# Two groups of eight heads instead of four groups of four for the products with values, and one copy for each

## The reference

```python
def _L0_xattn_ref(query, key, value, wq, wk, wv, wo):      # 16 heads of width 16
    q = (query @ wq.T).reshape(B, S, H, dk_h).transpose(0, 2, 1, 3)
    k = (key @ wk.T).reshape(B, S, H, dk_h).transpose(0, 2, 1, 3)
    v = (value @ wv.T).reshape(B, S, H, dv_h).transpose(0, 2, 1, 3)
    scores = jnp.einsum('bhqd,bhkd->bhqk', q, k) / scale
    attn = jax.nn.softmax(scores, axis=-1)
    out = jnp.einsum('bhqk,bhkd->bhqd', attn, v)
    out = out.transpose(0, 2, 1, 3).reshape(B, S, d_value)
    return out @ wo.T

x = x + jnp.tanh(g_xattn[0]) * _L0_xattn_ref(_layernorm(x), ctx_1024, ctx_1024, ...)
x = x + jnp.tanh(g_ffn[0]) * _L0_ffn_ref(_layernorm(x), ...)
x = x + jnp.tanh(g_xattn[1]) * _L1_xattn_ref(ctx_1024, _layernorm(x))    # an alignment by dynamic programming
x = x + jnp.tanh(g_ffn[1]) * _L1_ffn_ref(_layernorm(x), ...)
```

## Time and profile before

| | |
|---|---|
| median of 3 runs | 1828.75 us (1828.48 to 1829.92) |
| the profiled execution's own time | 1828.01 us |
| its span, first to last instruction | 1826.2 us |
| mean granted clock of TensorE over the span | 0.874 |
| busy in the span | PE 77%, DVE 78%, ACT 61%, POOL 30% |

### The profile page before, as it was taken

One profiled execution on the slowest core, in us unless ns is written; L12 is line 12 of the kernel. 1 busy time (PEld: TensorE's weight loads), 2 busy tenths in 40 slices (PEclk: granted clock), 3 DMA queues, 4 the chain that ended last, 5 costly groups with the idle time before them and its releaser, 6 DMA issues. The chain is left out here.

```text
span 1826.2 us, 35776 instructions
## 1 busy us (share of the span) xinstructions
PE 1414.0 (77%) x10821; PEld 1072.6 (59%) x10821; DVE 1420.9 (78%) x4062; ACT 1107.6 (61%) x2395; POOL 551.6 (30%) x998
## 2 busy tenths in 40 slices
PE   5899999999999999999999986133332004899896
PEld 4578788888887888878888765000001002566664
DVE  6677777777777777777777642899998998999996
ACT  3476676676766767667677662243335002999997
POOL 3122222322222223222233221200000002778785
PEclk8899999999999999999999997555555555999999
DMA  5444445444444444444543310322220002222321
GB/s 175 139 129 116 138 125 146 121 116 140 124 135 124 117 142 130 118 129 123 147 123 107 111 42 18 99 59 61 60 45 11 0 0 81 76 87 92 100 76 47
DMA packets 322936, 179.49 MB, mean 98 GB/s; under 512 B 93793, under 2 KB 318193, under 8 KB 322802
## 3 DMA queue, kind: packets, MB, share of 16 engines
q1 hardware_dynamic: 322802, 178.07, 35.0%
HBM read 122.91 MB, written 50.33 MB: 95 GB/s over the span
## 5 line engine op out<-in xcount | busy, mean ns | idle before, releaser
L982 DVE TENSOR_REDUCE nmax<-s 128x2 f32<-128x512 f32 x512 | 327.0, 681 | 7.9 <-PE s L454 6.9
L709 ACT ACTIVATE pt<-s 128x512 f32<-128x512 f32 x512 | 281.0, 611 | 70.0 <-PE s L471 69.9
L1074 POOL TENSOR_TENSOR r<-rl 128x512 f32<-128x512 f32 x128 | 133.1, 1040 | 328.4 <-ACT rl L739 285.6
L454 PE MATMUL s<-kst,qst 96*128 96x256 bf16 x1024 | 158.2, 275 | 11.6 <-DVE nmax L982 8.0
L471 PE MATMUL s<-qst,kst 128*128 128x256 bf16 x1024 | 156.9, 275 | 1.1 <-ACT pt L709 0.8
L1341 PE MATMUL gate<-diag,one 128*128 128x512 f16 x35 | 21.3, 608 | 171.7 <-DVE left L1432 171.7
L739 ACT ACTIVATE rl<-wb,fscl 128x256 f32<-128x256 f32 x256 | 107.8, 476 | 64.7 <-PE wb L555 64.7
L551 PE MATMUL wb<-x2l,wfcT 128*128 128x256 f32 x512 | 143.3, 302 | 0.7 <-ACT dd L761 0.7
L485 PE MATMUL oacc<-pt,vw 128*32 128x256 f32 x2048 | 137.0, 385 | 6.4 <-ACT pt L709 6.0
L951 DVE TENSOR_TENSOR r2l<-r,r2h 128x512 fp32r<-128x512 f32 x128 | 88.6, 692 | 65.2 <-POOL r L1074 40.3
L418 PE MATMUL wb<-wprT,r2l 128*128 128x256 f32 x512 | 131.8, 296 | 6.9 <-DVE r2l L951 6.9
(11 more groups left out here) (270 smaller groups left out, 3951.9 us busy)
## 6 DMA issues: line engine op xcount, KB each, us to landing
kst<-k_parts_dram SPq DMA_DIRECT2D x384, 64.0 KB, 2.5
qst<-q_parts_dram SPq DMA_DIRECT2D x384, 64.0 KB, 2.4
k_parts_dram<-kp SPq DMA_DIRECT2D x32, 384.0 KB, 5.2
q_parts_dram<-qp SPq DMA_DIRECT2D x32, 384.0 KB, 3.1
xin<-in_x_dram SPq DMA_DIRECT2D x32, 256.0 KB, 2.8
cT<-in_ctx_T_dram SPq DMA_DIRECT2D x32, 256.0 KB, 2.7
xres<-in_x_dram SPq DMA_DIRECT2D x32, 256.0 KB, 3.1
cin<-in_ctx_dram SPq DMA_DIRECT2D x32, 256.0 KB, 4.6
```

The costliest lines, as they stand in the source:

```text
L454: last = pe.matmul(s1[h % 2][:, t, :], qst[b.p][0:MAXROW, h, t * P:t * P + P], kst[b.p][0:MAXROW, h, :], start=True, stop=True)
L709: act.activation(pt[h % (2 * HPG)][:], s2[h % 2][:], ACT.Exp).then_inc(e["expd"], 1)
L982: v.tensor_reduce(nmax[:, T * h:T * h + T], s1[h % 2][:], AX.X, ALU.max, negate=True)\
L1074: pool.tensor_tensor(r2[:], rl[:, k % 2], rl[:, k % 2], ALU.mult)\
```

## The change

`values` takes eight heads at once: two groups of four, 16 matmuls (32 records) one after the other, into both halves of `oacc`. It is called twice in an iteration, where groups 1 and 3 stood; the calls for groups 0 and 2 are gone from their places. `copy_half` empties both halves of `oacc` with one instruction of 512 columns, where `copy_group(i, 1)` and `copy_group(i, 3)` stood. The semaphores' counts follow: the exponentials of a half of the heads wait for the products of the half that last used the `pt` tiles.

```diff
-            def values(b, g):
-
-                w("expd", NH * b.n + HPG * (g + 1), NH * NB)
-                if g == 0:
+            def values(b, half):
+                w("expd", NH * b.n + NH // 2 * (half + 1), NH * NB)
+                if half == 0:
                     if at(b, 0):
                         pe.wait_ge(e["w_made"], GPR_MADE)
                     w("vw_cp", b.n + 1)
-                w("o_cp", NG * b.n + g, NG * NB)
-                for t in range(T):
-                    for j in range(HPG):
-                        last = pe.matmul(oacc[HW * j:HW * j + HW, g % 2, :], vw[b.p][:, t, HPG * g + j, :],
-                                         pt[(HPG * g + j) % (2 * HPG)][:, t, :],
-                                         start=(t == 0), stop=(t == T - 1))
+                w("o_cp", 2 * b.n + half, 2 * NB)
+                for g in range(2):
+                    for t in range(T):
+                        for j in range(HPG):
+                            last = pe.matmul(oacc[HW * j:HW * j + HW, g, :], vw[b.p][:, t, NH // 2 * half + HPG * g + j, :],
+                                             pt[HPG * g + j][:, t, :], start=(t == 0), stop=(t == T - 1))
                 last.then_inc(e["av_mm"], 1)
...
                 if there(i):
-                    values(i, 0)
                     scores2(i, 4, 6)
...
                 if there(i):
-                    values(i, 1)
+                    values(i, 0)
...
                 if there(i):
-                    values(i, 2)
                     scores2(i, 14, 16)
...
                 if there(i):
-                    values(i, 3)
+                    values(i, 1)
...
             def exps(b, lo, hi):
                 for h in range(lo, hi):
                     w("s2_mm", NH * b.n + h + 1, NH * NB)
-                    w("av_mm", NG * b.n + h // HPG - 1, NG * NB)
+                    w("av_mm", 2 * b.n + h // (NH // 2), 2 * NB)
...
-            def copy_group(b, g):
-                w("av_mm", NG * b.n + g + 1, NG * NB)
-                w("o_t", 2 * (b.n - 1) + g // 2 + 1, 2 * NB)
-                act.activation(osb[:, g, :], oacc[:, g % 2, :], ACT.Copy).then_inc(e["o_cp"], 1)
+            def copy_half(b, half):
+                w("av_mm", 2 * b.n + half + 1, 2 * NB)
+                w("o_t", 2 * (b.n - 1) + half + 1, 2 * NB)
+                act.activation(osb[:, 2 * half:2 * half + 2, :], oacc[:], ACT.Copy).then_inc(e["o_cp"], 1)
```

More of the change, by code:

```diff
@@ L481, in values @@
                     w("vw_cp", b.n + 1)
-                w("o_cp", NG * b.n + g, NG * NB)
-                for t in range(T):
-                    for j in range(HPG):
-                        last = pe.matmul(oacc[HW * j:HW * j + HW, g % 2, :], vw[b.p][:, t, HPG * g + j, :],
-                                         pt[(HPG * g + j) % (2 * HPG)][:, t, :],
-                                         start=(t == 0), stop=(t == T - 1))
+                w("o_cp", 2 * b.n + half, 2 * NB)
[4 more added lines that the diff above has]
+                                             pt[HPG * g + j][:, t, :], start=(t == 0), stop=(t == T - 1))
                 last.then_inc(e["av_mm"], 1)
             def turn_o(b, half):
-                w("o_cp", NG * b.n + 2 * half + 2, NG * NB)
+                w("o_cp", 2 * b.n + half + 1, 2 * NB)
                 if half == 0:
@@ L698, in values_copy @@
                     act.wait_ge(e["pool_set"], VALUES_SET)
-                w("v_mm", b.n + 1), w("av_mm", NG * (b.n - 1), NG * NB)
+                w("v_mm", b.n + 1), w("av_mm", 2 * (b.n - 1), 2 * NB)
                 for t in range(T):
@@ L782, in iteration @@
                 if there(i):
-                    copy_group(i, 0)
                     exps(i, 4, 6)
@@ L797, in iteration @@
                 if there(i):
-                    copy_group(i, 1)
+                    copy_half(i, 0)
                 if there(y):
@@ L816, in iteration @@
                 if there(i):
-                    copy_group(i, 2)
                     exps(i, 14, 16)
@@ L822, in iteration @@
                 if there(i):
-                    copy_group(i, 3)
+                    copy_half(i, 1)
                 if there(z):
```

## The result

The changed kernel takes 1869.96 us (median of 4 runs, 1869.31 to 1874.01) against 1828.62 us before (4 runs, 1827.05 to 1829.92). The ratio is 1.0231, with a 95% interval of 1.0213 to 1.0249: slower, by 41 us. The prediction was 1871 us.

The account below looks back on a forecast made before the run. PE looked like the bound, but the moved groups were taken to fill its waits for DVE and ACT. +1.38 us a batch, 42.4 in all, on 1828.0 gave 1870.4; the median stands 0.7 higher, so 1871 us, range 1857 to 1878.

Parts of the forecast that it names:

- Price of a group and of a block: On PE: a group costs 1.11 us, 0.25 of it entering and leaving the narrow form; a 32-record block costs 1.93.
- First place: Group 0's old place, between queries and `scores2` of heads 4 and 5: PE waits for `yn` and `xh`, +0.52 us a batch.
- Second place: Group 2's old place, between heads 13 and 14: PE waits for ACT's exponentials, so removal gains 0.00 us a batch.
- The block at the end: Groups 2 and 3 joined where group 3 stood: same start, 0.86 us longer, later PE work shifts by +0.86 a batch.
- The sum: +1.38 us a batch, 38.6 over batches 2 to 29, 3.2 for 30 and 31, about +0.6 for 0 and 1: 42.4.
- Busy time: Sign: PE's busy time from 600 to 800 us falls to 94 or 96%, at a clock still 1.00.
- The first rival: Both places have slack and PE keeps what it is spared: 0.50 us less a batch, 1813 us; 5 in 100.
- The third rival: `copy_half` becomes exposed, `turn_o` or `distance` waits: up to 0.59 us a batch more, 1890 us; 4 in 100.

Follow-up runs that it names:

- The second merge alone: Kernel before, with only groups 2 and 3 joined in one block with one copy, groups 0 and 1 unchanged: 1855.12 us, ratio 1.0139.
- the copies alone: Kernel before, all four groups left in place, each two emptied by one 512-column copy behind the second: 1829.46 us, ratio 0.9997.
- the work done twice: Changed kernel, with heads 0 to 3 and 8 to 11 also multiplied at the places groups 0 and 2 left: 1881.53 us, ratio 1.0279.
- the block cut in two: Changed kernel, with heads 8 to 11 moved from the second block to ahead of `fc(z, 2)`, one copy kept: 1879.53 us, ratio 1.0295.
- the new order with one merge and with both: Groups 2 and 3 joined, or changed kernel with DVE's `yn` earlier; `fc(z, 2)` before scores of heads 14 and 15, other orders moved: 1827.46 and 1825.64 us.
- the earlier turn in each of these: Both reordered kernels, one merge and both, with `turn_x(a)` put ahead of `turn_o(z, 1)`: 1828.26 us with one, 1828.29 us with both.
- the four groups in the new order: Orders of the 1828.29 us kernel, with four groups and four copies, group 2 ahead of `fc(z, 2)`: 1842.77 us, ratio 1.0073.
- the kernel that met both: The 1828.29 us kernel (both merges, reordered, `turn_x` earlier), with DVE's `split_max(s)` moved behind `low_squares(z, 2)`: 1812.17 us, ratio 0.9910.
- two long blocks in the same new order: Changed kernel with DVE's `yn` and `xh` earlier, `fc(z, 2)` and other orders moved, and `turn_x` ahead of `turn_o`: 1828.29 us, ratio 0.9993.

## Why the prediction was right

It said 1871 us with a range of 1857 to 1878; measured were 1870.0. By its steps:

- *Price of a group and of a block.* A block of 1.93 us was forecast and measured. Going in and out was put at 0.25 us from one pair of neighbours; it is 0.31 between scores and `fc`. This had no weight in the 28 full batches, as PE had no use for the time.
- *First place, +0.52 a batch.* Measured alone: +0.54. The idle ahead of `turn_y` is 0.57 us (0.6 to 0.7 forecast, so a little less), released by DVE's line for `yn`. That DVE's chain wouldn't move, which carries this term, holds to 0.01 us. Batch 30, where PE was early already, gave the delays of 0.06 and 0.58 us; they came out at 0.05 and 0.59.
- *Second place, 0.00.* The stretch took 2.00 us and takes 1.98.
- *The block at the end, +0.86.* The second merge alone has +0.87.
- *The sum.* 1.38 a batch forecast, 34.33 - 32.93 = 1.40 measured, so the 28 full batches gave about 39 us for 38.6. The whole span grew by 41.2 where 42.4 were forecast. Laid side by side, the starts of the last group and of the last block of each batch split that: batches 0 and 1 cost nothing where +0.6 was forecast (105.31 + 0.86 after, against 106.15), batches 2 to 29 cost 39.1 for 38.6, batches 30 and 31 cost 3.2 for 3.2. When `proj` of the last batch but one begins, behind the last block, the change is 42.28 us late (1136.57 against 1094.29), so up to there the sum is right within 0.1, by two small misses that cancel. The rest was in no term. In the kernel before, this `proj` ran at the lower level of TensorE's clock (granted 0.52 on average), and in the changed one at the full clock. The last three numbers of these rows are the granted clock, the DMA share and GB/s; the first row is of the kernel before, the second of the changed one:

```profile
1094.30:1097.70 3.40, 3.40 (x16) 3.40 (x17) 0.00 (x0) 0.65 (x4) 0.00 (x0) 0.52 0.00 0
1136.60:1140.40 3.80, 3.80 (x32) 3.80 (x33) 0.00 (x0) 0.64 (x4) 0.00 (x0) 1.00 0.00 0
```

Both had the same waits of PE ahead of it (0.81 and 0.87 or 0.88 us), so why the clock differs isn't shown. It gives the changed kernel 1.5 us back: 16 records take 3.47 us before and 1.97 after, and the output projection behind them is 40.73 us late. The later phases add 0.5.
- *Busy time* from 600 to 800 us: 191.68 of 200, 96%, forecast 94 or 96.
- *The first rival* (PE keeps what it is spared, 1813 us) had PE's 99% for it. It fails on both places, and most plainly on the kernel that does half the products with values twice: about 71 us of work for 9 to 12 us of time.
- *The third rival* (the copy exposed) had for it the rule of the Trainium skill (Perfetto Trace Analysis, Optimizing Tensor Performance) that groups should rotate through PSUM banks. The page speaks of different banks, and here it is two halves of one tensor, so the rule bears on this change only by likeness. The trace of the changed kernel shows the room: the copy ends at 656.64 + 0.60 = 657.24, and `turn_o` starts at 657.81, which is the +3.17 of the prediction (657.81 - 654.64).

```profile
656.64 0.60 ACT L711 ACTIVATE osb<-oacc 128x512 f32<-128x512 f32 x1 [0.39 <-PE oacc L485]
...
657.81 0.60 PE L498 MATMUL wb<-ident,osb 128*128 128x128 f32 x4
```

The experiment with the copies alone shows no cost within 0.1%.

Where I was wrong was in the expectations of the experiments. Two lay 1.5 and 0.5 us above their ranges (the work done twice, the block cut in two). Five missed outright: the new order with one merge and with both, the earlier turn in each of these, and the four groups in the new order. Each rested on a list of waits that I had worked out, and each time one supplier was missing from it. The one behind the wait ahead of `proj` was an instruction that is ready, queued on DVE behind one that waits.

## What to carry to other kernels

A matrix engine that is 99% busy isn't proof that work taken from it is time gained: in a pipeline whose order is written by hand, a small group may stand where it fills the wait for a slower chain. Before moving a piece, look behind the place that it leaves: take the next instructions there, find when their inputs are ready, and count only the slack that is left. Joining small groups can bring its 0.25 to 0.4 us if both the place left behind has other ready work and nothing waits behind the longer block on any engine's queue; the kernel that met both, with other orders changed as well, is 0.9% faster, the one that met neither 2.3% slower. How much of the 0.9% the joining itself brings isn't shown.

## What the runs showed that I had not expected

- The price of going into the narrow form and out depends on the neighbours: 0.25 us between float32 matmuls and scores, 0.31 between scores and `fc`, where `fc` otherwise starts 0.36 us after the first of four scores. In the period the cut block costs 0.39 us; I can account for 0.33 of it (from the scores to the end block 2.90 us in place of 1.71, less the 0.86 by which that block is shorter).
- The view names one releaser for a wait, the one that ended last by the profile. Ahead of `proj` the copy of `xT` and DVE's `r2l` ended 0.1 us apart, and removing the named one gained nothing (ratios 0.9995 before the move and 0.9993 after).
- Four groups in the new order are 13 us slower than four groups in the old one, though two long blocks in the same new order are level with it: an order fits one grouping and not the other.
